# A vision tower on one core: the end of the attention overlapped with three tiles of the stage behind it

## The reference

```
h = h + attention(layernorm(h)) @ Wo.T      # 32 heads of 32, 8 key heads, causal, rotary positions
x = layernorm(h)
h = h + (q8(x) @ q8(w).T + b)               # q8: 8-bit rounding, scale per row of x and of w
```

## Time and profile before

| | |
|---|---|
| median of 3 runs | 1506.73 us (1504.13 to 1507.42) |
| the profiled execution, its own time | 1501.35 us |
| its span, first to last instruction | 1499.6 us |
| PE busy | 1427.6 us (95%) |
| DVE busy | 1196.9 us (80%) |
| POOL busy | 838.7 us (56%) |
| ACT busy | 733.8 us (49%) |
| mean granted clock of PE | 0.98 of full |

### The profile page before, as it was taken

One profiled execution on the slowest core, in us unless ns is written; L12 is line 12 of the kernel. 1 busy time (PEld: TensorE's weight loads), 2 busy tenths in 40 slices (PEclk: granted clock), 3 DMA queues, 4 the chain that ended last, 5 costly groups with the idle time before them and its releaser, 6 DMA issues.

```text
span 1499.6 us, 34041 instructions
## 1 busy us (share of the span) xinstructions
PE 1427.6 (95%) x10442; PEld 1111.9 (74%) x10442; DVE 1196.9 (80%) x2349; ACT 733.8 (49%) x2673; POOL 838.7 (56%) x894
## 2 busy tenths in 40 slices
PE   5999889999999999999999999769999999999997
PEld 3999867777777777777777777556777777777774
DVE  7888678889999999998999999676866666666665
ACT  6897566666766767676676767551000000000000
POOL 5796156667676767667676767422433334334342
PEclk8999999999999999999999999879999999999998
DMA  9356666667777777777767766865444344443441
GB/s 238 97 143 151 190 141 180 181 190 212 210 195 210 194 200 202 200 202 204 212 192 209 194 200 187 265 204 152 133 129 142 106 143 121 123 146 106 140 119 53
DMA packets 263402, 255.60 MB, mean 170 GB/s; under 512 B 73297, under 2 KB 201554, under 8 KB 263346
## 3 DMA queue, kind: packets, MB, share of 16 engines
q1 hardware_dynamic: 257586, 233.87, 56.2%
q10 hardware_dynamic: 5760, 21.04, 4.6%
HBM read 138.26 MB, written 106.57 MB: 163 GB/s over the span
## 4 chain that ended last, share of the span: by engine, by line
PE 82%; DVE 5%; POOL 5%; DMA 3%; issue 2%; ACT 1%; SPq 1%; ACTq 0%; DVEq 0%; POOLq 0%
PE att_ps L1097 35%; PE ffn_o L1703 23%; PE ffn_y L1794 8%; PE att_ps L1140 5%; PE att_ps L1152 4%; POOL yb L358 3%; PE att_ps L1129 2%; PE att_ps L1121 2%; POOL yb L364 2%; DMA p_blocks<-pB 1%; PE mix_ps L447 1%; PE att_ps L1108 1%; SPq L877 1%; DVE m L641 1%; DVE kb L542 1%
## 5 line engine op out<-in xcount | busy, mean ns | idle before, releaser
L1225 ACT ACTIVATE pr<-sm,ml 128x128 f32<-128x128 f32 x1024 | 399.1, 392 | 155.6 <-DVE ml L1400 155.6
L980 POOL TENSOR_TENSOR pr<-pr,ri 128x512 f32<-128x512 f32 x256 | 266.3, 1040 | 213.3 <-DVE ri L1407 206.0
L1097 PE MATMUL att_ps<-w_lo,xT_hi 128*128 128x512 f32 x776 | 319.6, 412 | 0.0
L1097 PE MATMUL att_ps<-w_hi,xT_hi 128*128 128x512 f32 x776 | 312.4, 403 | 4.4 <-DVE xT_lo L1348 3.6
L1097 PE MATMUL att_ps<-w_hi,xT_lo 128*128 128x512 f32 x776 | 307.4, 396 | 0.0
L1749 ACT CAST cT_hi<-ctx_in 128x512 fp32r<-128x512 f32 x64 | 36.4, 616 | 370.3 <-PE ffn_o L1703 360.8
L1703 PE MATMUL ffn_o<-wo_hi,cT_hi 128*128 128x512 f32 x528 | 212.5, 402 | 2.6 <-ACT wo_hi L1733 2.5
L1391 DVE TENSOR_TENSOR sm<-att_ps,cst 128x512 f32<-128x512 f32 x256 | 169.9, 664 | 52.3 <-PE att_ps L1140 52.3
L1703 PE MATMUL ffn_o<-wo_hi,cT_lo 128*128 128x512 f32 x528 | 206.6, 391 | 0.0
L1703 PE MATMUL ffn_o<-wo_lo,cT_hi 128*128 128x512 f32 x528 | 206.0, 390 | 0.0
L1225 ACT ACTIVATION_READ_ACCUMULATOR pr<-sm,ml 128x1 f32 x1024 | 193.4, 189 | 0.0
(11 more groups left out here) (207 smaller groups left out, 2396.1 us busy)
## 6 DMA issues: line engine op xcount, KB each, us to landing
pT<-p_blocks SPq DMA_DIRECT2D x256, 256.0 KB, 2.9
p_blocks<-pB SPq DMA_DIRECT2D x512, 64.0 KB, 2.0
h_rows<-ho SPq DMA_DIRECT2D x64, 256.0 KB, 3.7
ctx_turned<-ctxo SPq DMA_DIRECT2D x64, 256.0 KB, 3.2
h_in<-h_rows SPq DMA_DIRECT2D x32, 512.0 KB, 3.6
out_dram<-yo SPq DMA_DIRECT2D x32, 512.0 KB, 2.7
ctx_in<-ctx_turned SPq DMA_DIRECT2D x30, 512.0 KB, 3.6
hbuf<-h_rows ACTq DMA_DIRECT2D x29, 512.0 KB, 4.7
```

Of the source, the lines that this page charges most:

```text
L980: G.tensor_tensor(pr[:, g % 4], pr[:, g % 4], ri[:, g % 2, :].unsqueeze(2).to_broadcast([P, GQ, P]), ALU.mult).then_inc(p_ready, 1)
L1097: mm = nc.tensor.matmul(bank[:], x_part[:, t[1], e, tok:tok + P], w_part[blk][:, e, :], start=(r == 0), stop=(r == EC * 3 - 1))
L1225: a = nc.scalar.activation(pr[:, g % 4, q, :], sm[:, g % 2, q, :], ACT.Exp, bias=ml[:, b[1], 0, h:h + 1], accum_out=ml[:, b[1], 1, h:h + 1])
```

## The change

- **Wo earlier and in one burst.** Four loads of 1 MB (half the columns of four blocks each) instead of two of 2 MB: at steps 3, 5 and 7 of iteration 31 and at step 0 of iteration 32. The 16 rounds run eight each in steps 0 and 1 of iteration 32, on four PSUM banks.
- **First loads earlier.** `load_first` (0.5 MB three times on ACT's queue) moves from iteration 32 to step 0 of iteration 31.
- **Three tiles projected in the drain** instead of one: 12 parts of 12 matmuls (`project_ahead`), in steps 2 to 7 of iteration 32 and 0, 1, 4, 5, 6, 7 of iteration 33, ahead of `weigh(.., 1)`. The context tiles' high parts are on ACT (`upper_ahead`).
- **Low parts on POOL** (`lower_ctx`), for all tiles but the 33rd, in the drain (`lower_ahead`) and in the loop, where they stand ahead of `rstd`.
- **DVE's residuals of tiles 0 and 1 and the variance of tile 0** are done in the drain (`finish_ahead`).
- **SP's queue**: h of tile 1 and context of tile 2 are loaded in iteration 32, the DMA transposition of tile 0's `xq` at step 5 and of tile 1's at step 6 of iteration 33, ahead of the last context store; the scales are loaded behind the former.
- **Waits and places.** PE's wait for the last `ctx_ready` ahead of the second stage goes. The wait for `weighed` moves from ahead of the first `xq` to ahead of the first `scale_out`, since `xq` and `ya` have changed places in SBUF.

```diff
@@ wo_rounds_at @@
-        n = STEPS if at(t, NB + 1) else 0
-        return (2 * (s + n) - 2, 2 * (s + n) - 1) if at(t, NB) and s > 0 or at(t, NB + 1) and s == 0 else None
+        return range(8 * s, 8 * s + 8) if at(t, NB) and s < 2 else ()
@@ attention, sync, ends of steps @@
-            if at(t, NB):
-                load_scales(sp)
+                if at(t, NB) or at(t, NB + 1):
+                    load_ahead(sp, number(t) - NB, s)
@@ attention, tensor, in the steps @@
+                if at(t, NB) or at(t, NB + 1):
+                    for r in wo_rounds_at(t, s):
+                        turn_wo(pe, r, rot_ready, q_stored)
+                    project_ahead(pe, number(t) - NB, s)
                 if s == 7 and exists(c, NB):
                     weigh(c, 1)
...
-                if at(t, NB):
-                    if s == 0:
-                        pe.wait_ge(rot_ready, NBLK * (NB + 1))
-                    turn_wo(pe, 2 * s)
-                    turn_wo(pe, 2 * s + 1)
-                if at(t, NB + 1) and s > 0:
-                    project_first(pe, s)
@@ attention, scalar @@
+                if s == 0 and at(t, NB - 1):
+                    load_first(act)
                 if s == 0 and at(t, NB):
                     act.wait_ge(projected, NBLK * (NB + 1))
-                    load_first(act)
-                    load_wo(act, (1,))
-                    split_first(act)
+                    load_wo(act, 3)
...
-                if s == 3 and at(t, NB - 1):
+                if s in (3, 5, 7) and at(t, NB - 1):
                     act.wait_ge(projected, NBLK * nth(t) + 1)
-                    load_wo(act, (0,))
+                    load_wo(act, (s - 3) // 2)
...
+                for r in wo_rounds_at(t, s)[:4]:
+                    copy_wo(act, r)
                 d, g = group_at(t, s, 1)
                 if exists(d, NB):
                     exponentials(d, g)
+                for r in wo_rounds_at(t, s)[4:]:
+                    copy_wo(act, r)
+                if at(t, NB) or at(t, NB + 1):
+                    upper_ahead(act, number(t) - NB, s)
@@ second stage @@
+    def load_ahead(sp, i, s):
+        if (i, s) == (0, 2):
+            sp.wait_ge(rope_ready, NBLK * (NB + 1))
+            load_h(sp, (0, 1))
+        if (i, s) == (0, 3):
+            load_ctx(sp, (1, 0))
+        if (i, s) == (0, 6):
+            sp.wait_ge(scored, 2 * NB)
+            sp.dma_start(bias_sb[:], bias.rearrange("(a o) -> a o", a=1).to_broadcast([P, L])).then_inc(bias_in, 16)
+        if (i, s) == (1, 5):
+            turn_xq(sp, (0, 0))
+            load_ctx(sp, (1, 1))
+            load_h(sp, (1, 0))
+            sp.wait_ge(exp_done, 8 * NB)
+            sp.wait_ge(scales_out, 16)
+            sp.dma_start(w_scale[:], scale_dram.to_broadcast([P, L])).then_inc(scales_in, 16)
+        if (i, s) == (1, 6):
+            turn_xq(sp, (0, 1))
...
+    def lower_ahead(pool, i, s):
+        n = {(0, 1): (0, 0), (0, 4): (0, 1), (1, 0): (1, 0)}.get((i, s))
+        if n is not None:
+            for r in range(2):
+                lower_ctx(pool, nc.gpsimd, n, r)
+        if (i, s) == (0, 6):
+            inverse_deviation(pool, (0, 0))
...
+            if exists(n, NT) and not last_rows(n) and not (fixed(n) and number(n) < AHEAD + 1):
+                for r in range(2):
+                    lower_ctx(pool, nc.gpsimd, n, r)
...
-    def turn_wo(pe, r):
+    def turn_wo(pe, r, rot_ready, q_stored):
         b, f = divmod(r, EC)
-        if f == 0:
-            pe.wait_ge(wo_in[b], 16)
-        if r >= 2:
-            pe.wait_ge(wo_hi_done, r - 1)
-            pe.wait_ge(wo_lo_done, r - 1)
+        if f % 4 == 0:
+            pe.wait_ge(wo_in[r // 4], 16)
+        if r in (0, 3):
+            pe.wait_ge(rot_ready, NBLK * (NB + 1) - (1 if r == 0 else 0))
+        if r == 1:
+            pe.wait_ge(ctx_ready, 2 * (NB - 2))
+        if r == 2:
+            pe.wait_ge(q_stored, 2 * (NB - 1) + 1)
+        if r >= 4:
+            pe.wait_ge(wo_hi_done, r - 3)
+            pe.wait_ge(wo_lo_done, r - 3)
...
+    def project_ahead(pe, i, s):
+        n = {(0, 2): 0, (0, 3): 1, (0, 4): 2, (0, 5): 3, (0, 6): 4, (0, 7): 5, (1, 0): 6, (1, 1): 7,
+             (1, 4): 8, (1, 5): 9, (1, 6): 10, (1, 7): 11}.get((i, s))
+        if n == 0:
             pe.wait_ge(wo_hi_done, WO_ROUNDS)
             pe.wait_ge(wo_lo_done, WO_ROUNDS)
...
+            project(pe, divmod(t, 2), part * PER_HALF // 2, (part + 1) * PER_HALF // 2)
...
+    def upper_ahead(act, i, s):
+        n = {(0, 0): (0, 0), (0, 3): (0, 1), (0, 7): (1, 0)}.get((i, s))
...
-            if exists(t, NT) and not at(t, 0):
+            if exists(t, NT) and not (fixed(t) and number(t) < AHEAD):
                 project(pe, t, 0, 2 * PER_HALF)
...
-        pe.wait_ge(ctx_ready, 2 * NB)
...
+    def finish_ahead(v, i, s):
+        if (i, s) in ((0, 4), (0, 6)):
+            residual(v, (0, 0), (s - 4) // 2)
+        if (i, s) == (0, 6):
+            variance(v, (0, 0))
+        if (i, s) in ((1, 0), (1, 3)):
+            residual(v, (0, 1), s // 3)
```

More of the change, by code:

```diff
@@ L937, in sync, with gpsimd @@
         iterations(sp, body)
-    def gpsimd(pool):
+    def gpsimd(pool, lower_ahead):
         G = nc.gpsimd
@@ L1453, in body @@
                     scale_w(u)
[L1454 to L1458, removed]
+                for r in wo_rounds_at(t, s):
+                    lower_wo(v, r)
+                if at(t, NB) or at(t, NB + 1):
+                    finish_ahead(v, number(t) - NB, s)
         def cls_statistics():
@@ L1601, in load_first, with turn_xq @@
         load_ctx(sp, (0, 1))
[L1603 to L1608, removed]
-        sp.dma_start(bias_sb[:], bias.rearrange("(a o) -> a o", a=1).to_broadcast([P, L])).then_inc(bias_in, 16)
+    def load_ahead(sp, i, s):
[16 more added lines that the diff above has]
+            turn_xq(sp, (0, 1))
+    def turn_xq(sp, c):
+        if fixed(c) and number(c) < 2:
+            sp.wait_ge(xq_ready, number(c) + 1)
+        sp.dma_start(xqT[:, c[1]], xq[:, c[1], :], transpose=True).then_inc(xq_turned[c[1]], 16)
     def sync(sp):
@@ L1651, in sync @@
         for i in range(2):
-            sp.wait_ge(p_parted[i], 256 * NB)
-        load_h(sp, (0, 1))
-        for i in range(2):
             sp.wait_ge(ml_stored[i], 16 * NB // 2)
@@ L1679, in body @@
                 done.then_inc(biased, 1)
-            c = shifted(t, -1)
+            if at(t, 1):
+                for r in range(2):
+                    lower_ctx(pool, nc.gpsimd, (1, 1), r)
+                save_last_ctx()
             if exists(c, NT) and not last_rows(c):
@@ L1821, in body @@
             c, n = shifted(t, -1), shifted(t, 1)
-            if exists(n, NT) and not last_rows(n):
+            if exists(n, NT) and not last_rows(n) and not (fixed(n) and number(n) < AHEAD):
                 upper_ctx(act, n)
@@ L1830, in scalar, with residual, variance @@
         iterations(act, body)
+    def residual(v, t, half):
+        V = nc.vector
+        u = number(t)
+        cols = slice(half * BK, (half + 1) * BK)
+        if half == 0:
+            v.wait_ge(h_loaded[t[1]], 16 * (t[0] + 1))
+            at_least(v, biased, u - 1)
+        v.wait_ge(out_proj, 2 * u + half + 1)
+        V.tensor_tensor(h1[:, t[1], cols], O_BANK[half][:], h_in[t[1]][:, cols], ALU.add).then_inc(resid, 1)
+        v.wait_ge(resid, 2 * u + half + 1)
+        V.bn_stats(st[:, half, :], h1[:, t[1], cols]).then_inc(stats, 1)
+    def variance(v, t):
+        V = nc.vector
+        u = number(t)
+        v.wait_ge(stats, 2 * u + 2)
+        V.memset(gate[:], 0.0)
+        V.bn_aggr(mv[:], st[:].rearrange("p a b -> p (a b)")).then_inc(aggr, 1)
+        v.wait_ge(aggr, u + 1)
+        V.tensor_scalar(ve[:], mv[:, 1:2], 1e-5, None, ALU.add).then_inc(var_ready, 1)
+    def finish_ahead(v, i, s):
[5 more added lines that the diff above has]
+            residual(v, (0, 1), s // 3)
     def vector(v):
         V = nc.vector
[L1835 to L1852 removed]
         def quantise(t):
@@ L1946, in body @@
             c, n = shifted(t, -1), shifted(t, 1)
-            if exists(t, NT):
-                residual(t, 0)
-            if exists(n, NT) and not last_rows(n):
-                lower_ctx(v, n, 0)
-                lower_ctx(v, n, 1)
-            if exists(t, NT):
-                residual(t, 1)
-                variance(t)
+            if exists(t, NT) and not (at(t, 0) or at(t, 1)):
+                residual(v, t, 0)
+                residual(v, t, 1)
+            if exists(t, NT) and not at(t, 0):
+                variance(v, t)
             if last_rows(n):
-                lower_ctx(v, n, 0)
-                lower_ctx(v, n, 1)
+                lower_ctx(v, V, n, 0)
+                lower_ctx(v, V, n, 1)
             if exists(t, NT):
@@ L2012, in program @@
         raw_in = [sem(f"raw_in{i}") for i in range(NBLK)]
-        wo_in = [sem(f"wo_in{i}") for i in range(2)]
+        wo_in = [sem(f"wo_in{i}") for i in range(4)]
```

(9 more changed lines are left out.)

144 lines of the change are left out of this document (64 added, 80 removed).

## The result

The changed kernel takes **1489.51 us** (median of 4 runs, 1483.87 to 1493.45) where the kernel before takes 1505.78 beside it (4 runs, 1504.13 to 1507.42): a ratio of 0.989 (0.985 to 0.993). The profiled execution had 1493.45 us of its own, span 1491.6, against 1501.35 and 1499.6 before. So the two profiles show 8 us where the medians show 16; both have to be explained.

A forecast was written before the change was run, and what follows sets the result against it. PE, busy for 95% of the span, was taken as the bound. T0 7.7 us earlier plus 10.9 less work behind it, minus 2.4 given back, gain 16.2: 1490.5 us against 1506.73, own range 1485.5 to 1495.5, stated range 1484 to 1501.

The forecast's parts named there:

- Work behind T0: PE work left once the first dense layer starts: 30 projections instead of 31, so 10.91 us less.
- T0: Moment the first dense layer starts, at the drain's end: forecast from 1031.9 to 1024.2, 7.7 us earlier.
- Start: PE's turning of the last q, ahead of the Wo burst: carried over unchanged, with -3 to +8 us.
- The sign named under what would make the prediction wrong: Between 938 and 965, ahead of the Wo burst: DVE standing on block DMAs for more than 5 us.
- Wo rounds: Burst after the last q: PE sets the pace at low clock, eight rounds to 972.6, DVE's subtractions to 981.3.
- Low clock of the first projections, 2.0: In the drain: the first nine or ten projection matmuls follow at 0.43 us instead of 0.23, costing 2.0 us.
- Waits, 1: In the drain ahead of the first dense layer: 1 us added for PE waits that could not be placed.
- The rival that this chain still holds T0: End of drain: masks, exchange, `weigh` or first `xq` hold PE to 1031.9; gain only 8.5 us, 1498.2; chance 0.12.
- Low parts on POOL, 0: Second-stage loop: two subtractions, 2.6 us per tile, fit POOL's idle 5.94 ahead of `rstd`; cost nothing, 0 to +4.
- the rival made of it: Second-stage loop: POOL becomes the bound; at 7.5 us per pair it loses 1.6 per tile, 1535 us; chance 0.04.
- Hand-over, 2.4 given back: First iterations behind the first dense layer: PE idles 1.3 and 1.1 us, 2.4 given back (0 to 4).
- turned by DMA in 4.4: In the hand-over: tile 2's `xq`, ready at T0 + 15.5, is transposed in 4.4 us, at T0 + 19.9.

The follow-up runs named there:

- first loads late: Changed kernel with the second stage's first loads (1.5 MB on ACT's queue) back in iteration 32: 1488.29 us, ratio 0.989.
- two tiles ahead: Changed kernel with only tiles 0 and 1 projected in the drain and tile 2 behind it: 1496.53 us, ratio 0.995.
- scores first: Changed kernel with the scales loaded ahead of context and h, and end_scores ahead of the first scale-out, its load early: 1491.76 us, ratio 0.992.
- small stores late: Changed kernel with the four 96 KB stores of the last context rows one iteration later, behind tile 2's transposition: 1485.62 us, again 1488.53.
- the versions that add to it: Late small stores plus early scales and end_scores (1487.67 us), plus first loads in iteration 32 (1487.69), or plus all of these (1487.80).
- the repeat: Changed kernel timed once more, unchanged: 1490.72 us, ratio 0.990 to the kernel before.

## Why the prediction was right, and where it wasn't

The time came out as forecast, 1489.51 for 1490.5. By its steps:

- **Work behind T0, -10.91:** as said; from dense 3 on nothing differs (423.7 and 423.7).
- **T0 7.7 earlier:** 7.8 in this profile, 8.2 as a mean of eleven with three tiles ahead (M + 104.5) against two of before (112.7). It is the right sum of terms that were off both ways. *Start:* I carried it over with a stall of 2 to 5 us; DVE stood for 9.3 and q was turned at M + 46.7 instead of M + 43.8, so 2.9 late. With the first loads late it is M + 43.7 to 44.2, in the other profiles of the changed order 46.0 to 48.5, so it is the early first loads that cost this. The sign named under what would make the prediction wrong (over 5 us of stall) did appear, but its price was 2.9 us and not 8.2, for PE had other work. *Wo rounds:* 17.3 us from the turning of q to their end by my working, 16.5 measured. DVE set the pace (its `wo_lo` ended the waits of 2.02 and 1.72) and not PE, whose later rounds ran at full clock (0.63 for four transposes); the sum came out near all the same. *Low clock of the first projections, 2.0:* not there; they start at 0.23 us per matmul. *Waits, 1:* 0.3 here, and 0.2 to 1.7 over the eleven, ahead of the `weigh` at about M + 90.
- **Chain of the last tile:** no wait of PE for the last `weigh` in any of the eleven profiles with three tiles ahead, and the first `xq` is turned before T0. The rival that this chain still holds T0 is out. It shows with two tiles ahead (8.61 us idle), so the third tile's 10.9 us of matmuls are what covers it, as the prediction said. They cost little ahead of T0 for it: with two tiles T0 is only some 2 us earlier, counted from M.
- **Low parts on POOL, 0:** right from both sides. 2.53 for the pair (forecast 2.6), 3.4 us left (3.3), and the same time with the pair on DVE. The Trainium skill's rule (SBUF — State Buffer, on SBUF's two separate sides) on a shared pair of ports speaks against such a move, and the rival made of it lost 1.6 us a tile. The trace shows no blocking: the two subtractions take 2.53 together, as two of POOL's `hb` do (1.29 each), and a tile is no longer. But it does not test the rule either: DVE idles 4.02 us while they run, waiting for PE, as the prediction's argument against the rival had it. No run here sets them beside DVE's long operations.
- **Hand-over, 2.4 given back: this term was mis-sized.** It was 8.0, then 6.6. The wait of 1.09 ahead of dense 1 stood in no term: tile 0's `xq` was ready at T0 - 6.8 instead of T0 - 9.2 and tile 1's behind it at T0 - 0.9 instead of T0 - 3.7, and its transposition took 5.6. The two parts that I worked out from DVE's order were nearly right (residual of tile 2 at T0 + 8.1 for 8.2, `xq` at T0 + 15.9 for 15.5). The step that failed is "turned by DMA in 4.4": I took the price of a transposition from a row that had no small stores ahead of it. Before, the stores are issued from 1042.59 and the next transposition at 1053.37, 10.8 us later; now 8.2 us lie between them, since no projection of tile 2 stands there any more. It takes 6.5, PE idles 2.8 instead of 1.1, and in the five profiles where it idled 2.76 to 3.69 the dense layer then ran below full clock (0.50 to 0.61 over its first 3 to 4 us): 5.2 to 6.6 us for 3.63. That the stores are the cause is shown by moving them alone: the seven profiles with them 3.2 to 4.9 us ahead (from the end of their issue) have 6.4 to 8.0, the five with them behind 4.2 to 4.4, and what is given back falls to 2.4 and 2.5, the number of the prediction. The kernel before had them ahead too, but 7.5 us. The rows suggest how: the load of context behind the stores lands 8.6 to 8.9 us after its issue instead of 4.0 to 4.4, so in the changed kernel it is still under way for the first 4.0 us of the transposition, with scores first for 5.8 and with two tiles ahead for 5.4 (6.5, 8.0 and 7.8 to land), but before for 0.5 (4.3). Whether the transposition is slowed by that load or by the stores themselves no run here separates.
- **Why the median fits all the same.** With 7 to 8 given back, the terms make 8.2 + 10.9 - 7.3 = 11.8 us, and the two profiles of each kernel differ by 10.2 in the mean of their own times, but the medians by 14 to 16. The profiled executions of before were 1 to 4.5 us under its medians, those of the changed kernel 0.5 to 4 above theirs. M alone wanders from 917.7 to 924.3 over the fourteen profiles, in code that is the same in all. Some 3 us of the medians' difference can't be placed from the profiles; that stays open. So part of the hit is luck: a gain of 16.2 was forecast with a hand-over some 5 us too cheap.

The best version is the one with the small stores late: 1485.62 and 1488.53 in its two groups of runs; the versions that add to it (1487.67 to 1487.80) can't be told from it. It is below the changed kernel in both, by 5.1 and by 1.0 against 1490.72 and 1489.51, which were timed in other groups, and its gain over before is 16 to 19 us. Its lead over the changed kernel is 4 to 5 us in the traces' hand-over, and 2.7 with 2.7 either way in the times.

## What to carry to other kernels

When an edit takes PE work out between two stages, list what each DMA queue issues in that stretch: things that were 11 us apart may now be 8 apart, and a transfer that was priced from the old trace can be half as long again. Move the transfers that nobody waits for behind the one that PE waits for; the longest wait in the rows (4.74 us for the scales) may be worth nothing, while four stores that no wait names are worth 4 to 5 us in the traces. And count from a mark ahead of the change before comparing two profiles: here 2.8 us of the difference came from code that had not changed.

## What the hardware showed that I had not expected

- A DMA transposition issued 3.2 to 4.9 us behind the last of four stores of 96 KB took 6.4 to 8.0 us to land instead of 4.2 to 4.4, and its issue on SP's queue 1.5 to 3.0 instead of 1.24. At 7.5 us distance it took 4.3. A load of 512 KB between them took 8.6 to 8.9 instead of 4.0 to 4.4, although the DMA engines were busy for only 0.31 of the time (50 GB/s) in most of that stretch of the changed kernel.
- One idle stretch of 2.8 us on PE was followed by a dense layer of 16 matmuls at 0.50 of full clock, in 6.56 us instead of 3.63, 5.31 in the repeat; after 2.65 us of idling it ran in 3.63.
- Stretches of the same code moved by up to 6.6 us between executions (M 917.7 to 924.3), more than the effect of most edits here.
